# A projection group moved one step earlier in the attention loop of a fused GNN, attention and expert kernel

## The reference

```
h = _ln(x, ln1_g, ln1_b)
q = jnp.einsum('btd,hds->bhts', h, Wq)
k = jnp.einsum('btd,hds->bhts', h, Wk)
v = jnp.einsum('btd,hds->bhts', h, Wv)
scores = jnp.einsum('bhts,bhus->bhtu', q, k) * d ** (-0.5)
scores = jnp.where(causal, scores, -jnp.inf)
att = jax.nn.softmax(scores, axis=-1)
out = jnp.einsum('bhtu,bhus->bhts', att, v)
x = x + out.transpose(0, 2, 1, 3).reshape(b, t, d) @ Wp + bp
```

## Time and profile before

| | |
|---|---|
| median of 3 runs | 883.43 us (883.32 to 887.26) |
| the profiled execution's own time | 885.82 us |
| its span, first to last instruction | 884.2 us, mean granted clock 0.991 |
| busy: PE, PEld | 850.2 us (96%), 819.3 us (93%) |
| busy: DVE, ACT, POOL | 715.1 us (81%), 552.2 us (62%), 78.2 us (9%) |
| attention steps | from about 225 to about 375 us of the span |
| transfers | 196.00 MB, mean 222 GB/s, dense only in the expert layer (from about 418 us) |

### The profile page before, as it was taken

The page is one execution under the profiler, slowest core; times in us unless marked ns, Lnnn a source line. Parts: engine busy times, 40 slices in busy tenths (PEclk is TensorE's granted clock), DMA queues, the critical chain, the costliest instruction groups (busy, mean ns, idle before and its releaser), DMA issues.

```text
span 884.2 us, 14643 instructions
## 1 busy us (share of the span) xinstructions
PE 850.2 (96%) x5336; PEld 819.3 (93%) x5336; DVE 715.1 (81%) x1095; ACT 552.2 (62%) x785; POOL 78.2 (9%) x85
## 2 busy tenths in 40 slices
PE   7999999989899998999989999999999999999997
PEld 7889999989789887899979999999999999999996
DVE  6999675873578788665887897998989899898995
ACT  4612342353577777614577787888878788787870
POOL 2000000230400000031600000000000000000040
PEclk9999999999999999999999999999999999999997
DMA  7030008153930033430898999999999999999974
GB/s 218 23 108 1 19 6 174 54 154 75 321 110 2 1 107 103 148 88 1 273 363 309 364 347 375 343 363 372 354 376 359 364 372 357 376 354 372 368 260 130
DMA packets 116232, 196.00 MB, mean 222 GB/s; under 512 B 34052, under 2 KB 83420, under 8 KB 116182
## 3 DMA queue, kind: packets, MB, share of 16 engines
q1 hardware_dynamic: 107988, 169.08, 56.6%
q0 software_dynamic: 6368, 24.19, 8.0%
q10 hardware_dynamic: 1826, 2.06, 0.9%
HBM read 177.40 MB, written 17.90 MB: 221 GB/s over the span
## 4 chain that ended last, share of the span: by engine, by line
PE 56%; DVE 21%; DMA 12%; ACT 5%; issue 5%; SPq 0%; DVEq 0%; ACTq 0%
PE ps L1486 12%; DVE wlo L994 11%; DMA raw<-in_L_ffn_W 11%; PE ps L1900 10%; PE ps L1881 9%; PE ps L1663 7%; PE ps L1739 3%; PE ps L1717 2%; PE ps L1567 2%; PE ps L1593 2%; PE ps L1702 2%; ACT whi L664 2%; PE ps L1515 2%; PE ps L1866 1%; DMA xs<-in_x 1%
## 5 line engine op out<-in xcount | busy, mean ns | idle before, releaser
L994 DVE TENSOR_TENSOR wlo<-raw,whi 128x2304 fp32r<-128x2304 f32 (+1 forms) x150 | 352.8, 2360 | 21.6 <-ACT whi L664 20.9
L664 ACT ACTIVATE whi<-raw 128x2304 fp32r<-128x2304 f32 (+1 forms) x152 | 300.7, 1979 | 82.4 <-DMA raw<-in_L_ffn_W 30.6
L1900 PE MATMUL ps<-whi,hTT 128*128 128x384 f32 x768 | 202.7, 340 | 1.0 <-ACT oh7T L664 1.0
L1900 PEld LDWEIGHTS ps<-whi,hTT 128*128 128x128 f32 x768 | 140.3, 189 | 1.2 <-ACT oh7T L664 1.2
L1881 PE MATMUL ps<-whi,hgh 128*128 128x384 f32 x384 | 133.2, 347 | 1.3 <-DVE hgl L994 1.3
L1900 PE MATMUL ps<-wlo,hTT 128*128 128x384 f32 x384 | 129.7, 338 | 0.0
L1881 PE MATMUL ps<-whi,hgl 128*128 128x384 f32 x384 | 129.1, 336 | 0.0
L1881 PE MATMUL ps<-wlo,hgh 128*128 128x384 f32 x384 | 128.4, 334 | 0.0
L1881 PEld LDWEIGHTS ps<-whi,hgh 128*128 128x128 f32 x384 | 72.2, 188 | 1.5 <-DVE hgl L994 1.5
L1900 PEld LDWEIGHTS ps<-wlo,hTT 128*128 128x128 f32 x384 | 72.8, 190 | 0.0
L1881 PEld LDWEIGHTS ps<-wlo,hgh 128*128 128x128 f32 x384 | 72.3, 188 | 0.0
(11 more groups left out here) (291 smaller groups left out, 1627.6 us busy)
## 6 DMA issues: line engine op xcount, KB each, us to landing
raw<-in_L_ffn_W SPq DMA_DIRECT2D x128, 1152.0 KB, 6.9
hs_d<-bc POOLq DMA_DIRECT2D x13, 384.0 KB, 6.4
raw<-in_L_gnn_W SPq DMA_DIRECT2D x4, 1152.0 KB, 6.3
hs<-hs_d POOLq DMA_DIRECT2D x8, 384.0 KB, 5.5
ys_d<-ysb POOLq DMA_DIRECT2D x7, 384.0 KB, 6.0
raw<-in_L_ffn_Wv SPq DMA_DIRECT2D x6, 384.0 KB, 5.4
raw<-in_L_ffn_Wq SPq DMA_DIRECT2D x12, 192.0 KB, 3.7
raw<-in_L_ffn_Wk SPq DMA_DIRECT2D x12, 192.0 KB, 3.4
```

Of the source, the lines that this page charges most:

```text
L664: act.activation(out_, in_, func).then_inc(s, 1)
L994: dve.tensor_tensor(out_, in_, hi_, ALU.subtract).then_inc(s, 1)
L1900: ins = mm(ps[0:CAP, 4 + half, 0:HB], l, rr, start=k == 0 and j == 0 and jj == 0, stop=k == FCH - 1 and j == JW - 1 and jj == 2)
```

## The change

Group 1 of each next pair, the second half of its q, moves from the steps with i % 5 = 1 to those with i % 5 = 0. One table holds the order for PE, ACT and DVE, so the products (L1663) and both readings (`qk_out` on ACT and DVE) move together. The order of the groups stays 0, 1, 2, 3. Steps 0, 5, 10, 15 and 20 gain a group, and steps 1, 6, 11, 16 and 21 lose it; the last pair's own steps have no groups.

```
-QK_LATE = {4: 0, 1: 1, 2: 2, 3: 3}
+QK_LATE = {4: 0, 0: 1, 2: 2, 3: 3}
```

## The result

| | before | after |
|---|---|---|
| median | 883.43 us (9 runs, 877.76 to 887.26) | 891.95 us (9 runs, 887.57 to 898.75) |
| ratio | | 1.0088, 95% interval 1.0061 to 1.0116 |
| run again later, beside before on one chip | 885.53 us (22 runs) | 891.01 us (11 runs), ratio 1.0056 (1.0033 to 1.0080) |
| profiled execution: its own time, span, granted clock | 885.82, 884.2 us, 0.991 | 898.17, 896.1 us, 0.984 |

The changed kernel is slower by 0.6 to 0.9% (the ratios are estimates of their own and not the quotients of the medians, which are 1.0096 and 1.0062). Its profiled execution is one of its slowest: the spans of its nine executions go from 885.9 us at a mean granted clock of 0.996 to 897.1 us at 0.984.

The account below looks back on a forecast made before the run. PE was taken to set the attention's pace, with DVE's cover thin. Losses of 1.0 + 0.65 + 0.65 + 2.07 + 1.96 = 6.3 us (pairs 0 to 4) on the median 883.43 gave 889.7, range 885.6 to 894 us.

Parts of the forecast that it names:

- PE in the first step: Steps gaining the group: 18 products cost 2.69 us, less a covered 0.27 in pairs 1 to 3, nothing covered in pair 4.
- T': End of the last turning (L1724) in a pair's first step after the change.
- T: End of the last turning (L1724) in a pair's first step before the change.
- The stop in the second step: PE ahead of the values of block 4, waiting for DVE's readings: 0.51 us later in pair 2, loss 1.96 in pair 4.
- DVE's way: DVE from the last turning to the next pair's scores: T' + 14.17 in pairs 1 and 2, T' + 15.91 in pair 3.
- A sign that I had named: Stop ahead of the next pair's scores: from 0.78 to above 2 us after pair 3, the others to about 0.5.
- Pair 0: First pair: the group waits until DVE has read group 0, delaying the turning in step 2; loss taken as 1.0 us.
- The sum: Losses of pairs 0 to 4 together: 6.3 us, added to the median 883.43 for a forecast of 889.7.
- the clock: Rival: new stops of near 2 us lower PE's clock, two falls priced at 3 us in all, 892.7; chance 0.06.
- The smaller loss: Rival: DVE and ACT catch up before the low part of k is wanted; 3.2 us, 886.6; chance 0.17.
- the faster case: Rival: PE is the only limit and the group covers stops; 2.1 us faster, 881.3; chance 0.07.
- the larger loss: Rival: DVE's way binds in every pair, pairs 1 and 2 losing 2.07 each; 9.1 us, 892.6; chance 0.12.

Follow-up runs that it names:

- pair 4 alone: Kernel before with group 1 moved in pair 4 only (step 21 to step 20); 885.79 us against 884.65 before, ratio 1.0020.
- heads first: Changed kernel, but in a pair's first step ACT and DVE read the heads of block 3 ahead of the moved group; 886.76 us in one execution, before beside it 881.94.
- its early form: Changed kernel with the last turning right behind the moved group, ahead of the values of block 3, in pairs 1 to 4; 887.46 us against 884.65 before, ratio 1.0031.
- The experiment with the split of step 18: Changed kernel with the weight split of step 18 moved to step 19, behind the next pair's first scores; 893.35 us in one execution.
- filling the stops: Changed kernel with 5 and 6 products that compute nothing in its two long stops (after pair 3, in pair 4); 887.78 us against 885.53 before, ratio 1.0037.
- the best order tried: Kernel before with the group moved in pairs 1 and 2 only, the last turning right behind it there; 884.16 us against 883.90 before, ratio 0.9992.
- removed (10): Changed kernel with both weight splits moved, step 20 to 21 and step 18 to 19; 888.00 us against 883.90 before, ratio 1.0040.

## Why the prediction was right, point by point

**PE in the first step.** Predicted T' = T + 2.42 in pairs 1 to 3. In pair 2 the last turning ended at 282.68, 11.09 behind the pair's start, and before at 8.76 behind it: 2.33. The small stop ahead of the values of block 3 was covered as said, and the group did not wait for the reading of group 0. In pair 4 the term was too large: T' - T is 2.44 (pair 4 alone: 330.14 - 319.06 = 11.08 behind the pair's start, and before 8.64), where I had 2.69. I had taken it that nothing there could be covered. But the last turning of before took 0.48 us there and 0.38 elsewhere, a lateness that I had not read in the row; where the rest of the 0.25 went no run shows.

```profile
329.76 0.38 PE L1734 MATMUL ps<-ident,pr 125*125 125x125 f32 x2
```

**The stop in the second step.** Predicted at T' + 1.98, measured 284.64 - 282.68 = 1.96. The last pair of the kernel before, with the same order and no group, was the row to take it from the earlier trace rows. The values of pair 4 were predicted at T' + 3.18 and start at T' + 3.19 (333.33 - 330.14, pair 4 alone). The terms held one by one: the group's reading 0.39 against 0.40 (heads first), the split's share of pair 4 1.21 (1.77 against 0.56) against 1.2, and the last turning as the point of release (its early form).

**DVE's way.** Predicted T' + 14.17 in pairs 1 and 2, measured 296.76 - 282.68 = 14.08. In pair 3 predicted T' + 15.91, measured 323.57 - 307.86 = 15.71. That pair's loss is 1.78 for 2.07, since both T' - T (2.33) and the way were each 0.1 to 0.2 shorter. The experiment with the split of step 18 gives the way its price: 0.88 for 0.87. A sign that I had named did not come: the stop ahead of the scores behind pair 3 was to grow above 2 us and grew to 1.59, and the ones behind pairs 1 and 2 to about 0.5 and stayed at 0.35. In these two pairs DVE's way and PE's own are equally long, so the loss there (0.47 and 0.51 for 0.65) is that of the stop in the second step.

**Pair 0.** 1.04 for 1.0. Group 1 waited for the reading of group 0 (1.34 us), and the turning in step 2 for ACT.

**The sum.** 5.6 us at full clock against 6.3 predicted: every term but pair 0's was 0.1 to 0.3 too large. The forecast of 889.7 lies 2.2 below the median of the first nine executions; in the later runs the medians are 5.5 us apart, 0.8 less than predicted. That it came so near is in part luck: my terms were 0.7 too high in sum, and the clock, which the forecast left out, lay on the other side in the first nine.

**The rivals.** The smaller loss is excluded by pair 3, the faster case by the stops of 0.56, the larger loss by pairs 1 and 2. The clock was given 0.06, as a case beside the forecast. It came on top of the forecast, in some executions, and this is where the prediction fell short: "no row of the attention shows it" was true, but the stops that I had worked out myself (1.8 and near 2 us) were longer than any between the attention's products in the rows (1.25), so the rows of before could not speak against it. My price of 3 us for two falls was right for this trace (2.9 in pair 4, with a third of 1.39 in pair 5); in the mean over executions, filling the stops gives back 2.6 us, with an error of 0.8. What the Trainium skill says ("TensorE: Matmul & The Clock Gate", section "Part 1: The HAM clock gate"), that idleness takes the clock to half its level, agrees with these traces: 0.50 in the windows behind the stops of 1.59 and 1.77 us. The rule on the weight loads' busy share ("Trainium Kernel Development and Optimization", "Best Practices"), by which PE would have had 2.3 us of room in a pair, found no support here: the best order tried won 0.45 in pairs 1 and 2, about the stops that the timeline showed. That no other order would win more is not shown.

**What stays open.** Why the clock falls behind one stop and not behind another of the same length, and how much of the loss against the kernel before is the clock's in the mean.

## What to carry to other kernels

In a loop whose engines hand results on through strict queues, a block of matmuls is also the cover for the readings behind the block ahead of it. Before moving it, list what is released at the end of its old and its new neighbours, and measure each chain of readings against the cover that is left; here a chain of 1.96 us met a cover of 1.3. An engine that is 20% idle can still set the pace of one pair: what counts is its unbroken way from the point that releases it to the result that is waited for, and each small task on that way has its full price (a split of 0.87 us, taken off the way of pair 3, gave back 0.88). Taking away one stop gives back only what the next longest way allows: in pair 4 the stop fell by 1.21 us and the pair by 0.46, and pair 5 behind it by 0.4. When an edit makes new stops of TensorE, price the clock too, and look at the granted clock and the spans of many executions before comparing two traces.

## What the runs showed of the hardware that was not expected

Behind five of ten stops of 1.59 to 1.78 us between dense products TensorE's granted clock went to its half level (0.50). In pair 5, with stops of about 0.8, 0.4 and 0.7 us close together, it did so too in four of the thirteen traces. All four are of kernels with a longer stop ahead, and in three of them the clock had fallen once before, at the stop of pair 4. Not one of the six traces without a stop above 1.35 us shows a fall in the attention. In such a stretch products of 314 columns start 0.27 us apart and not 0.15, and one fall makes a pair 1.3 to 1.5 us longer. The changed kernel's mean granted clock was 0.9905 (19 executions); with the stops filled (12) or removed (10) it was 0.9932 and 0.9930, and in the kernel before 0.9916, 0.9925 and 0.9928 in its three sets of runs. Within the changed kernel's first nine executions 0.001 of mean clock went with 0.93 us of span, about the 0.89 us (0.001 of 890) that it costs when TensorE is the limit throughout.
